# Reordering the lead of a cross-attention kernel: bias, key quads and context loads

## The reference

```python
def _L0_xattn_ref(x, y, wq, bq, wk, bk, wv, bv, wo, bo):    # 16 heads of 16
    q = x @ wq.T + bq
    k = y @ wk.T + bk
    v = y @ wv.T + bv
    ...
    score = jnp.einsum('bhqd,bhkd->bhqk', q, k) * scale
    attn = jax.nn.softmax(score, axis=-1)
    out = jnp.einsum('bhqk,bhkd->bhqd', attn, v)
    ...
    return out @ wo.T + bo
...
x = x + _L0_xattn_ref(_layernorm(x, axis=-1), ctx_768, ...)
```

## Time and profile before

| | us |
|---|---|
| median of 3 runs | 1296.68 (1294.81 to 1300.5) |
| the profiled execution | 1298.86 |
| its span on the core | 1297.1 |
| TensorE busy | 1235.7 (95%) |
| VectorE, ScalarE, GpSimd busy | 864.0, 718.5, 256.0 |
| TensorE's mean granted clock | 0.978 of full speed |

### The profile page before, as it was taken

How to read it: one execution, slowest core, us unless ns; L and a number is a source line. 1 busy time by engine, 2 the same in 40 slices (tenths; PEclk the granted TensorE clock), 3 DMA queues, 4 the chain that set the end, 5 groups by cost and what they waited for, 6 DMA issues and landing times.

```text
span 1297.1 us, 29481 instructions
## 1 busy us (share of the span) xinstructions
PE 1235.7 (95%) x12130; PEld 703.3 (54%) x12130; DVE 864.0 (67%) x1662; ACT 718.5 (55%) x942; POOL 256.0 (20%) x254
## 2 busy tenths in 40 slices
PE   8969999999999999999999999999999988999994
PEld 5444444455544455544445554444556567687774
DVE  5958888676788867688886767993355775232233
ACT  4537777766677867677776767787433321121120
POOL 4411211211111211111211112102012232222210
PEclk9979999999999999999999999999999996999997
DMA  7463474344355553344653433501000006999983
GB/s 225 86 90 50 73 140 95 58 65 60 58 89 142 78 73 61 50 56 99 132 77 50 57 50 56 88 13 51 8 2 2 2 34 242 416 411 397 390 343 110
DMA packets 47621, 148.32 MB, mean 114 GB/s; under 512 B 16816, under 2 KB 20928, under 8 KB 39552
## 3 DMA queue, kind: packets, MB, share of 16 engines
q1 hardware_dynamic: 43232, 134.57, 43.9%
q0 software_dynamic: 2528, 7.38, 1.7%
q10 hardware_dynamic: 1728, 4.49, 1.0%
HBM read 87.68 MB, written 5.24 MB: 72 GB/s over the span
## 4 chain that ended last, share of the span: by engine, by line
PE 86%; ACT 4%; DVE 3%; issue 2%; DMA 2%; POOL 1%; SPq 1%; ACTq 0%; DVEq 0%; POOLq 0%
PE psum L626 21%; PE psum L608 15%; PE psum L586 10%; PE psum L519 6%; PE psum L500 6%; PE psum L1052 5%; PE psum L1080 4%; ACT wts L1125 2%; PE psum L1077 2%; PE psum L1046 2%; PE psum L704 2%; PE psum L824 1%; SPq L1971 1%; DMA keys<-key_low 1%; PE psum L698 1%
## 5 line engine op out<-in xcount | busy, mean ns | idle before, releaser
L1375 DVE TENSOR_REDUCE part_max<-psum 128x1 f32<-128x512 f32 x952 | 610.0, 686 | 165.3 <-PE psum L586 163.8
L1125 ACT ACTIVATE wts<-psum 128x1024 f32<-128x1024 f32 x512 | 515.6, 1023 | 91.9 <-PE psum L608 90.7
L626 PE MATMUL psum<-wts,vals 128*17 128x256 f32 x4096 | 317.3, 385 | 0.0
L608 PE MATMUL psum<-queries,keys 51*128 51x256 f32 x2048 | 261.1, 333 | 8.2 <-ACT wts L1125 7.0
L608 PEld LDWEIGHTS psum<-queries,keys 51*128 51x128 f32 x2048 | 158.2, 185 | 199.8 <-issue 141.1
L586 PE MATMUL psum<-keys,queries 51*128 51x512 f32 x1024 | 228.8, 443 | 16.9 <-DMA keys<-key_low 8.8
L626 PEld LDWEIGHTS psum<-wts,vals 128*17 128x17 f32 x4096 | 69.6, 95 | 120.3 <-issue 96.1
L586 PEld LDWEIGHTS psum<-keys,queries 51*128 51x128 f32 x1024 | 97.4, 185 | 35.4 <-DVE part_max L1375 9.7
L1802 POOL CAST key_high<-key_low 128x1024 fp32r<-128x1024 f32 x31 | 32.1, 1037 | 389.4 <-ACT key_low L1132 385.2
L519 PE MATMUL psum<-wv,ctx_in 64*128 64x256 f32 x768 | 102.0, 395 | 3.0 <-ACT vals L1138 2.9
L1295 ACT ACTIVATE hid<-psum,b1s 128x128 f32<-128x128 f32 (+1 forms) x124 | 31.6, 350 | 112.6 <-PE psum L1052 76.2
(11 more groups left out here) (243 smaller groups left out, 1011.2 us busy)
## 6 DMA issues: line engine op xcount, KB each, us to landing
keys<-key_high SPq DMA_DIRECT2D x256, 128.0 KB, 4.3
w1s<-in_W SPq DMA_DIRECT2D x31, 1024.0 KB, 10.3
w2s<-in_W SPq DMA_DIRECT2D x31, 1024.0 KB, 11.1
keys<-key_low SPq DMA_DIRECT2D x128, 128.0 KB, 6.2
ctx_in<-in_ctxT SPq DMA_DIRECT2D x12, 768.0 KB, 8.9
ctx_in<-in_ctxT ACTq DMA_DIRECT2D x4, 768.0 KB, 12.5
queries<-query_high SPq DMA_DIRECT2D x60, 32.0 KB, 4.7
rows_x<-xn SPq DMA_DIRECT2D x2, 512.0 KB, 2.6
```

The costliest lines, as they stand in the source:

```text
L608: m = e.matmul(bank(S_BANKS[S_NO["s", n] % 2] + i)[:, hh * SEQ:(hh + 1) * SEQ], keys[64 * i:64 * i + STK, hh, c, at:at + P], queries[g % 3 ...
L626: i = e.matmul(bank(O_BANK)[32 * j:32 * j + VW, 0:SEQ], vals[:, t, h * VW:(h + 1) * VW], wts[n % NW][:, j * SEQ:(j + 1) * SEQ], start=(t = ...
L1125: i = e.activation(wts[n % NW], s_bank(job, 2), ACT.Exp, scale=QSCALE)
L1375: e.reduce_max(part_max[g % 2][:, hq, c:c + 1], bank(M_BANKS[n % 3]), AX_X).then_inc(dve_max, 1)
```

## The change

Seven things: the keys of quad 1 become the first job of the planned lead instead of standing ahead of it; quad 2 goes ahead of the second query job; value job 11 leaves the lead for step 1; the planner starts one step later and takes 830 units a step; ScalarE issues quarters 2 and 3 of the context behind its load of the first queries; its norm of the six later row tiles comes without quad 1's eviction ahead of it; and GpSimd adds the bias after the jobs of step 0.

```diff
-LEAD_JOBS = [("v", 0, 4), ("v", 0, 5), ("v", 0, 6), ("turn1", 0), ("turn1", 1), ("q", 0), ("v", 0, 7), ("q", 1), ("k", 2),
-             ("v", 0, 8), ("v", 0, 9), ("v", 0, 10), ("k", 3), ("v", 0, 11)]
+LEAD_JOBS = [("k", 1), ("v", 0, 4), ("v", 0, 5), ("turn1", 0), ("turn1", 1), ("v", 0, 6), ("q", 0), ("k", 2), ("v", 0, 7),
+             ("q", 1), ("v", 0, 8), ("v", 0, 9), ("k", 3), ("v", 0, 10)]
-PER_STEP = 800
+PER_STEP = 830
...
-    pieces, ends, spent = {}, {}, 0
+    pieces, ends, spent = {}, {}, PER_STEP
...
-FIRST_AT.update((2 * j - 23, [("v", 0, j)]) for j in range(12, KT // 2))
+FIRST_AT.update((2 * j - 21, [("v", 0, j)]) for j in range(11, KT // 2))
...
-S_JOBS = [("k", 0)] + [("v", 0, _j) for _j in range(FIRST_V)] + [("k", 1)]
+S_JOBS = [("k", 0)] + [("v", 0, _j) for _j in range(FIRST_V)]
...
# TensorE
-            keys_of(1)
...
# ScalarE
-            for p in range(NCH // 2):
+            for p in range(2):
                 e.dma_start(ctx_in[:, p], a["ctxT"][0, p]).then_inc(ld_ctx[p], 16)
...
             load_q(e, 0)
+            for p in range(2, NCH // 2):
+                e.dma_start(ctx_in[:, p], a["ctxT"][0, p]).then_inc(ld_ctx[p], 16)
             first_queries(1)
...
             key_ones(slot(6))
-            empty(("k", 1))
             e.wait_ge(dve_root1, 1)
...
# GpSimd
-            split_keys(1)
...
-                        e.wait_ge(ld_w, 16 * 4)
-                        e.wait_ge(dve_rows1, BT)
-                        e.wait_ge(act_rows1, TT - BT)
-                        add_bias(range(TT), bo_bc)
...
+                if n == 0:
+                    e.wait_ge(ld_w, 16 * 4)
+                    e.wait_ge(dve_rows1, BT)
+                    e.wait_ge(act_rows1, TT - BT)
+                    add_bias(range(TT), bo_bc)
...
# SP
-            scatter_k(1)
```

## The result

The changed kernel takes 1302.72 us (median of 20 runs, 1299.3 to 1308.05). The kernel before takes 1296.47 (20 runs, 1293.73 to 1302.54). The ratio, taken over all the runs and not from the two medians, is 1.0043, with a 95% interval of 1.0031 to 1.0056: 0.4% slower, where 1292.2 was forecast. The median also lies above the forecast's range, which ended at 1299.0.

What follows compares the result with a forecast made beforehand. Bound: TensorE, over nine tenths busy, with an 8.8 us hole for quad 2's keys. Pair 32 sooner - 4.9, clock - 0.8, value job + 1.25: - 4.45, so 1292.2 us; eight in ten from 1288.5 to 1299.

Steps and rivals of the forecast that it cites:

- C: Time both late context quarters have landed: issue at 21.3 plus 8.9 us gives 30.2, ends 28.1 and 32.2.
- TensorE's wait for them: New wait ahead of quad 1's first piece, for the late context quarters: 3.6 us, with the whole lead behind it.
- quad 1's pieces, from C to eviction: Three key pieces on TensorE after C, 1.0 + 1.45 + 1.45 us, so eviction starts at 34.1.
- wait at pair 16: Second wait, for quad 1's keys landing at 50.0: VectorE could start at 49.3, can at 50.6; 1.3 us.
- eviction to keys landed: A quad's chain from ScalarE's eviction through cast and scatter to landing, without the bias in between: 15.9 us.
- wait at pair 32: The 8.8 us wait for quad 2's keys goes, with 0.9 us to spare: landing 70.3, VectorE there at 71.7.
- both late: Queues taking turns by packets: context loads and scatter both end late, near 32.2, and the gain is 2 us smaller.
- The case of no wait for the context: Rival: context landed by 27, all 3.0 us sooner, - 7.45 us, 1288.7 to 1289.7; chance 0.25.
- The clock case: Rival: clock falls in the context wait, lead runs slower, + 4.5 us, 1296.7 to 1298.7; chance 0.15.
- third-quad-late rival: Rival: quad 2's keys still late at pair 32, up to 4 us of wait return, 1292.2 to 1296.2; chance 0.08.
- The clock term: Without the 8.8 us hole, a pair and a value job run at the upper clock level, 2.0 for 2.8 us: - 0.8.
- the value job: One value job more in steps 1 to 9, where TensorE sets the pace: + 1.25 us.

Runs made afterwards that it cites:

- weights_late: Changed kernel with SP's third group of queries and four small weights issued behind quad 1's scatter; 1304.17 us, ratio 1.0055 to the kernel before.
- ctx_sp: Changed kernel with the two late context quarters issued by SP, behind quad 0's scatter in the same queue; 1302.28 us, ratio 1.0027 to the kernel before.
- ctx_mid: Changed kernel with the two late context quarters issued by ScalarE ahead of its query transfers, at 13.2 and 13.6; 1298.66 us, ratio 0.9995 to the kernel before.
- after_again: The changed kernel once more, with no edit, for a second trace; 1301.03 us, ratio 1.0028 to the kernel before.
- bias_only: Kernel before with one edit, the bias additions moved behind the jobs of step 0; 1292.95 us, ratio 0.996 to the kernel before.
- keep_warm: Changed kernel with 20 unused filler matmuls on TensorE in the wait for the late context; 1302.07 us, ratio 1.0032 to the kernel before.
- quad2_only: Kernel before with one edit, quad 2 ahead of value job 7 and the second query job; 1291.14 us, ratio 0.9948 to the kernel before.
- ctx_early: Changed kernel with all four context quarters issued at the start, as before the change; 1294.2 us, ratio 0.9978 to the kernel before.
- bias_quad2: Kernel before with quad 2 ahead of value job 7 and the second query job, and the bias behind step 0; 1293.28 us, ratio 0.9963.

## Why the prediction was wrong

The kernel is slower because transfers of 1.5 MB in all were moved from the start, where no engine stood for them, to a time when the first keys and queries need the DMA engines. Point by point:

| step | forecast | measured in after |
|---|---|---|
| C, both late quarters landed | 30.2 | 34.3 |
| TensorE's wait for them | 3.6 | 7.98 |
| quad 1's pieces, from C to eviction | 3.9 | 5.8 |
| quad 1 evicted | 34.1 | 40.20 |
| eviction to pair 16 | 15.9, and a pair's 0.5 | 15.96 |
| wait at pair 16 | 1.3 (VectorE) | 2.32 (VectorE 2.43) |
| quad 2 evicted | 54.35 | 60.65 |
| eviction to keys landed | 15.9 | 16.02 |
| pair 32 on VectorE | 71.7 | 77.81 |
| wait at pair 32 | none | 0.27 |
| quad 4's keys, step 12 | 99.3 | 104.48 |

**The step that failed is the landing of the context, term C.** It was forecast for 30.2 and came at 34.3. It was priced at the 8.9 us median of the earlier trace rows with 32.2 as its upper end, and it measured 13.8 us. In the earlier trace rows a context quarter is behind a scatter late in the stream; here two quarters, quad 0's scatter and the queries were all on their way at once. The view of the DMA queues (packets, MB, share of the 16 engines) of after at 21 to 23 us, and then at 25 to 27, shows what was different:

```profile
q1 hardware_dynamic: 75, 0.24, 97.2%
q10 hardware_dynamic: 67, 0.04, 14.6%
```

```profile
q10 hardware_dynamic: 105, 0.65, 92.3%
```

q1 is SP's queue, q10 ScalarE's. While both have work they move nearly the same number of packets, but ScalarE's are small ones, its own query transfers, which stand ahead of the context. When SP's queue is empty, at 25 to 27, the context moves at 0.65 MB in 2 us. At 27 to 29 SP's queue works again, and the context moves at less than half of that:

```profile
q10 hardware_dynamic: 65, 0.30, 77.5%
q1 hardware_dynamic: 63, 0.19, 27.5%
```

What SP's queue moves there is still quad 0's scatter: in weights_late, where nothing else of SP is on its way, the same view has 66 and 63 packets. That the queues take turns by packets is the rule of the Trainium skill that the prediction weighed (DMA: Bandwidth & Descriptors, on queues, rings and completion order). Those packet counts agree with it, and its side, "both late", came true, later still than the upper end. ctx_sp showed that the end is the same with the order reversed; ctx_mid, that an earlier start pays with the keys. The case of no wait for the context, at 0.25, was wrong by the same step.

**The clock case came true inside it.** It was to decide when C went past about 31; C was 34.3. It got a chance of 0.15, because C itself had been put too early. Its size, 3.7 us for the pieces from 2.8 us steps, was too large for this trace: the clock was back shortly after 38, before the third piece, so 5.8 instead of 3.9, + 1.9. In after_again, where it stayed down for all three, it was 7.3, + 3.4, nearly the forecast's size. The delay of C (+ 4.2 at TensorE's restart) and this make the + 6.1 at quad 1's eviction; the same 6.1 is there at pair 32 on VectorE (77.81 to 71.7), without loss or gain between. (The forecast's own terms add up to 71.8, not 71.7.) The longer wait at pair 16 belongs to this: VectorE went through pairs 4 to 15 at 1.14 us each, not 1.227, and only waited longer for the same landing.

**What was right.** The chain from eviction to landing held at 16.0 us twice. Quad 2 is in time for pair 32 with little to spare, as forecast, so the third-quad-late rival (0.08) did not happen. The bias additions (81.32 to 86.85) delayed nothing that this trace shows. bias_only bore out the removal of that wait as the forecast had it: 5.3 us off the 8.8.

**The clock term and the value job** were put at - 0.8 and + 1.25 between pair 32 and step 12. From VectorE's pair 32 to quad 4's keys it was 27.06 us in before and 26.67 in after: - 0.4 instead of + 0.45. The timeline of TensorE separates the two terms, by the rows in after that answer to the earlier trace rows:

```profile
83.43 0.50 PE L586 MATMUL psum<-keys,queries 51*128 51x512 f32 x2 [1.33 <-DVE part_max L1375]
...
84.88 0.59 PE L608 MATMUL psum<-queries,keys 51*128 51x256 f32 x4
```

The pair and the value job took 1.45 us, where before had 2.80 at the lower level: - 1.35, not - 0.8, because the forecast gave them 2.0 at the upper one. From there to step 12 it is 19.60 instead of 18.45, + 1.15 for the value job, near the + 1.25. The last - 0.2 lies ahead of these rows, where the forecast had nothing.

**The sum.** - 4.45 forecast; + 6.1 for the late context and the clock within it, - 0.85 for the last item: + 0.8. Measured at step 12 it is + 0.79, and in the profiled times + 0.44.

**From + 0.44 to + 6.25.** The medians differ by 6.25, and 5.8 of it is not in the two profiles. It is 3.4 for after's profile being fast and 2.4 for before's being slow. For the first there is a mechanism in the lead, from other runs that have after's lead with small edits. In after and after_again quad 2 is evicted 20.45 us after quad 1. In weights_late, keep_warm and ctx_sp, where the clock fell again at pair 16's wait of 2.4 to 2.9 us, it is 23.6 to 23.9: 3.1 to 3.4 more. From pair 32 on TensorE to step 12 it is 27.8 and 27.9 us in the first two, and 29.3 to 29.4 where the clock fell once more, at 86 to 88. Together that is some 5 us, and the three profiled runs with both took 1303.3 to 1304.4. That the slower of after's 20 runs are of this kind is argued from their mean clocks (0.970 to 0.971 at 1306.6 to 1308.05, 0.979 at 1299.3), not shown, as they have no trace. It also has a rival: the stretch from step 12 to the end of the span takes 1190.1 us in bias_only and quad2_only, 1193.0 in after and 1196.2 in ctx_mid, and the clock differs there too. These are the windows of 900 to 1000 us in quad2_only, after and ctx_mid (the clock is the third number from the end):

```profile
900.00:1000.00 100.00, 97.11 (x1035) 57.35 (x1035) 48.97 (x101) 38.72 (x66) 12.71 (x18) 1.00 0.02 3
```

```profile
900.00:1000.00 100.00, 97.72 (x961) 55.87 (x960) 47.36 (x98) 38.38 (x62) 10.18 (x14) 0.98 0.02 3
```

```profile
900.00:1000.00 100.00, 97.11 (x900) 55.68 (x902) 43.95 (x91) 35.95 (x58) 8.54 (x13) 0.95 0.02 3
```

So single executions differ by up to 6 us behind step 12 as well, with no edit there, and a mean clock does not tell in which part a run without a trace lost its time. How the 5.8 us divide between the two stays open, and so does why before's profile was slow in its turn. What needs no such division is that the late context costs time in the medians.

**Which part does what** (medians). Late context: + 6.8 in the company of the others (after_again against ctx_early, 1301.03 to 1294.2), + 11.1 alone (1308.88 to 1297.81). All the rest: - 0.2% (ctx_early). Quad 2 ahead of the queries alone: - 0.5% (quad2_only). So the rest of the change, with quad 1 in pieces, the bias moved and another value job behind the lead, adds nothing to that one edit; the two were run beside different sets of before, and their intervals only just touch, so that it costs something is likely and not shown. The gain that the prediction saw is real and is had by moving one job; quad2_only, at 1291.14 against 1297.81 for before on its chip, beats both kernels.

## What to carry to other kernels

Before moving an early load behind something urgent, add up the bytes and packets that stand ahead of it in its queue or take turns with it, and price its landing from that, not from the same load in a quiet place. When two edits remove the same wait, try each alone: the second may bring only a new wait. And a wait of a few microseconds on TensorE is to be priced with its chance of a slower clock behind it: equal executions of one kernel differed in it here. For the same reason a gain in one trace is to be read at a point just behind the edit, and not only from the span.

## What the runs showed of the hardware

- The granted clock fell 5 us after the last matmul in before, some 3 us after it in bias_only (the wait that ended at 70.49 began at 67.0, and it fell just before 70), and 1.5 us in after. In ctx_early it fell around 28 with no pause over 2.14 us ahead of it. It stayed down 10.2 us in after, 17.1 in bias_only and 6.8 in quad2_only. In after_again it still stood at the upper level at 29, when TensorE's wait had begun at 27.9, but it had come back from an earlier low stretch only at about 26.4.
- Low stretches of the clock came in places that no edit touched, and not alike in every trace: the mean of 900 to 1000 us was 1.00 in quad2_only, 0.98 in before and after and 0.95 in ctx_mid.
- The two late context quarters let TensorE go on at the same time whether ScalarE's queue issued them beside quad 0's scatter (34.41) or SP's queue behind it (34.35).
- Beside quad 0's scatter and the queries the 16 DMA engines moved 139 GB/s at 21 to 23 us in after, with their time fully taken; with loads alone it was 423.
- Tiny instructions of VectorE grew from 0.18 to 1.6 us beside one long instruction of GpSimd. TensorE, which waited for them, stood 3.46 us in bias_quad2.
